# Aggregation of a graph layer: gathered rows become the stationary operand, one-hots of 80 nodes the moving one

## What is computed

```
deg     = max(segment_sum(1, dst), 1)                 # edges per node, first block
agg[v]  = sum over edges e with dst[e] = v of  ew[e] * table[src[e], :]
wdeg[v] = sum over edges e with dst[e] = v of  ew[e]  # weights per node
```

## Time and profile before

| | us |
|---|---|
| median of three runs | 3854.28 |
| span of the profiled execution | 4334.5 |
| PE busy in it | 2842.8 (66%) |
| POOL busy | 2524.5 (58%) |
| DVE busy | 1865.2 (43%) |
| ACT busy | 795.6 (18%) |
| first aggregation, from the first gather on | 106 to 1271 |
| second | 1815 to 2971 |
| third | 2977 to 4185 |

### The profile page before, as it was taken

The page is one execution under the profiler, slowest core; times in us unless marked ns, Lnnn a source line. Parts: engine busy times, 40 slices in busy tenths (PEclk is TensorE's granted clock), DMA queues, the critical chain, the costliest instruction groups (busy, mean ns, idle before and its releaser), DMA issues. The chain is left out here.

```text
span 4334.5 us, 42515 instructions
## 1 busy us (share of the span) xinstructions
PE 2842.8 (66%) x12338; PEld 2151.9 (50%) x12338; DVE 1865.2 (43%) x5797; ACT 795.6 (18%) x1977; POOL 2524.5 (58%) x2689
## 2 busy tenths in 40 slices
PE   3577767777777566646656656555476767767678
PEld 2455545555544544435545545444354555555557
DVE  6343446666646823513322222222244444444443
ACT  1111101111113223301111111100022222232230
POOL 4666666666630533666666666665666666666601
PEclk9788879888888788978878778776788888888878
DMA  5333334444432466634333333332333333333305
GB/s 156 101 111 105 108 94 121 124 128 118 120 90 87 151 200 196 208 108 119 116 101 108 108 108 107 102 98 82 89 107 108 106 107 110 103 110 109 104 21 180
DMA packets 279543, 501.74 MB, mean 116 GB/s; under 512 B 59771, under 2 KB 179969, under 8 KB 279162
## 3 DMA queue, kind: packets, MB, share of 16 engines
q0 software_dynamic: 126240, 345.85, 27.7%
q1 hardware_dynamic: 135916, 139.10, 10.4%
q10 hardware_dynamic: 17136, 13.84, 1.0%
HBM read 419.12 MB, written 79.18 MB: 115 GB/s over the span
## 5 line engine op out<-in xcount | busy, mean ns | idle before, releaser
L1401 POOL DMA_INDIRECT g<-d_t,src_i x1568 | 1506.9, 961 | 806.4 <-issue 483.4
L1473 PE MATMUL bank<-g,m 128*128 128x256 f32 (+1 forms) x4704 | 1440.7, 438 | 94.3 <-issue 45.4
L1473 PEld LDWEIGHTS bank<-g,m 128*128 128x128 f32 x4704 | 943.0, 221 | 307.3 <-issue 141.2
L1401 POOL DMA_INDIRECT g<-d_xn,src_i x784 | 766.0, 977 | 389.2 <-issue 223.7
L1426 DVE TENSOR_SCALAR m<-iota,rel_f,ew_f 128x128 f32<-128x128 f32 x2352 | 702.0, 362 | 383.3 <-DMA d_xs<-zero 170.3
L1461 PE MATMUL bank<-ident,s 128*128 128x128 f32 x588 | 144.0, 334 | 438.3 <-ACT s L1407 390.2
L1437 DVE TENSOR_TENSOR accT<-bank,accT 128x256 f32 x294 | 121.9, 415 | 628.8 <-remote 269.8
L1407 ACT ACTIVATE s<-bank 128x256 f32<-128x256 f32 (+1 forms) x294 | 111.7, 380 | 1338.4 <-DMA nb<-d_deg 435.6
L1461 PEld LDWEIGHTS bank<-ident,s 128*128 128x128 f32 x588 | 86.3, 166 | 495.2 <-ACT s L1407 425.9
L1425 DVE TENSOR_SCALAR eq<-iota,rel_f 128x128 bf16<-128x128 f32 x784 | 227.5, 290 | 182.9 <-remote 140.3
L1435 DVE TENSOR_TENSOR dinv<-bank,dinv 2x128 f32 x98 | 27.1, 276 | 319.4 <-remote 310.0
(11 more groups left out here) (386 smaller groups left out, 4235.9 us busy)
## 6 DMA issues: line engine op xcount, KB each, us to landing
g<-d_t,src_i POOLq DMA_INDIRECT x1568
side_xn<-d_xn SPq DMA_DIRECT2D x96, 256.0 KB
g<-d_xn,src_i POOLq DMA_INDIRECT x784
d_swT<-wkv SPq DMA_DIRECT2D x48, 256.0 KB
swT<-d_swT SPq DMA_DIRECT2D x24, 512.0 KB, 3.7
xt<-d_xs POOLq DMA_DIRECT2D x80, 128.0 KB, 2.9
d_ys<-y ACTq DMA_DIRECT2D x80, 128.0 KB, 2.5
x<-in_x SPq DMA_DIRECT2D x24, 256.0 KB, 2.8
```

The source lines that it names most:

```text
L1401: pool.indirect_dma_start(g[n % RING][:, u, 0:D], None, table, bass.IndirectOffsetOnAxis(ap=k.src_i[:, t:t + 1], axis=0)).then_inc(gathere ...
L1473: ins = pe.matmul(b[:, 0:GW], m[o][:, u, :], g[r][:, u, :], start=(u == 0), stop=(u == GT - 1 and not count))
```

## The change

With the roles of the operands swapped a product forms features x nodes directly. `g` is stationary, in two halves of 128 features, and the one-hot moves, 80 nodes wide (WIN = 80). Both halves of the sum and the two rows of counts stand side by side in one bank, [0:80], [80:160] and, in the first aggregation, rows 0 and 1 of [160:240]. The counts come from two narrow stationary tiles: `first_row` (fp32, column 0 is one) with the moving `m`, `second_row` (bf16, column 1 is one) with the moving `eq`. Banks 0, 1 and 7 take turns, so PE may be two groups ahead of DVE's `finish`. ACT's copy, PE's transposes, the tiles `s` and the ones in `g` are gone; `finish` waits for the group's own products and adds straight from its bank.

```diff
--- before.py
+++ after.py
@@ -27,7 +27,8 @@
 AW = D + 2
-WIN = 128
+WIN = 80
+ACCS = (0, 1, 7)
...
@@ -1362,20 +1363,18 @@
 
     k = kit
     RING, ONEHOTS = 4 if count else 5, 3
-    GW = D + 1 if count else D
-    SW = GW + 1 if count else D
     with Stage(nc, kit) as st:
         side = side_of(st, a, d)
-        g = [st.sb(f"g{r}", [P, GT, GW]) for r in range(RING)]
-        m = [st.sb(f"m{r}", [P, GT, P]) for r in range(ONEHOTS)]
-        eq = [st.sb(f"eq{r}", [P, GT, P], BF16) for r in range(ONEHOTS)] if count else []
-        s = [st.sb(f"s{h}", [P, SW]) for h in range(2)]
+        g = [st.sb(f"g{r}", [P, GT, D]) for r in range(RING)]
+        m = [st.sb(f"m{r}", [P, GT, WIN]) for r in range(ONEHOTS)]
+        eq = [st.sb(f"eq{r}", [P, GT, WIN], BF16) for r in range(ONEHOTS)] if count else []
+        first_row, second_row = (st.sb("first_row", [P, 2]), st.sb("second_row", [P, 2], BF16)) if count else (None, None)
...
         gathered = [[st.pool_dma(f"gathered{r}_{h}") for h in range(2)] for r in range(RING)]
-        m_done, multiplied, copied, window_turned, acc_added, ones_set = (
-            st.sem(n) for n in ("m_done", "multiplied", "copied", "window_turned", "acc_added", "ones_set"))
+        m_done, multiplied, acc_added, rows_blank, rows_set = (
+            st.sem(n) for n in ("m_done", "multiplied", "acc_added", "rows_blank", "rows_set"))
@@ -1401,17 +1400,7 @@
                     pool.indirect_dma_start(g[n % RING][:, u, 0:D], None, table, bass.IndirectOffsetOnAxis(ap=k.src_i[:, t:t + 1], axis=0)).then_inc(gathered[n % RING][u // 4], 16)
 
         def main_act(act):
-            def copy(n):
-                wait(act, multiplied, 2 * (n + 1))
-                wait(act, window_turned, n - 1)
-                act.activation(s[n % 2][:], k.bank[n % 2][:, 0:SW], ACT.Copy).then_inc(copied, 1)
-            for i in range(ROUNDS):
-                for slot in range(2 * GT):
-                    if slot == 1 and 0 < i <= NB:
-                        copy(2 * i - 1)
-                    if slot == 9 and i < NB:
-                        copy(2 * i)
-                    at_step(side.act, slot, i)
+            sides(side.act)
 
         def main_dve(dve):
             def prepare(n):
@@ -1422,23 +1411,26 @@
                 for u in range(GT):
                     t = n * GT + u
                     if count:
-                        dve.tensor_scalar(eq[r][:, u, :], k.iota[:], k.rel_f[:, t:t + 1], None, ALU.is_equal)
-                    ins = dve.tensor_scalar(m[r][:, u, :], k.iota[:], k.rel_f[:, t:t + 1], k.ew_f[:, t:t + 1], ALU.is_equal, ALU.mult)
+                        dve.tensor_scalar(eq[r][:, u, :], k.iota[:, 0:WIN], k.rel_f[:, t:t + 1], None, ALU.is_equal)
+                    ins = dve.tensor_scalar(m[r][:, u, :], k.iota[:, 0:WIN], k.rel_f[:, t:t + 1], k.ew_f[:, t:t + 1], ALU.is_equal, ALU.mult)
                 ins.then_inc(m_done, 1)
 
             def finish(n):
                 base = dve.value_load(k.base_i[0:1, n:n + 1], min_val=0, max_val=N)
-                wait(dve, window_turned, n + 1)
+                window = k.bank[ACCS[n % 3]]
+                wait(dve, multiplied, 2 * (n + 1))
                 wait(dve, acc_added, n)
                 if count:
                     to = k.dinv[0:2, bass.ds(base, WIN)]
-                    dve.tensor_tensor(to, k.bank[7][0:2, D:D + WIN], to, ALU.add)
+                    dve.tensor_tensor(to, window[0:2, C * WIN:(C + 1) * WIN], to, ALU.add)
                 at = k.accT[:, :, bass.ds(base, WIN)]
-                dve.tensor_tensor(at, chunks(k.bank[7]), at, ALU.add).then_inc(acc_added, 1)
+                dve.tensor_tensor(at, window[:, 0:C * WIN].rearrange("p (c n) -> p c n", c=C), at, ALU.add).then_inc(acc_added, 1)
             if count:
-                for r in range(RING):
-                    ins = dve.memset(g[r][:, :, D:D + 1], 1.0)
-                ins.then_inc(ones_set, 1)
+                dve.memset(first_row[:], 0.0).then_inc(rows_blank, 1)
+                dve.memset(second_row[:], 0.0).then_inc(rows_blank, 1)
+                dve.wait_ge(rows_blank, 2)
+                dve.memset(first_row[:, 0:1], 1.0).then_inc(rows_set, 1)
+                dve.memset(second_row[:, 1:2], 1.0).then_inc(rows_set, 1)
             prepare(0)
             prepare(1)
             for i in range(ROUNDS):
@@ -1452,27 +1444,21 @@
                     at_step(side.dve, (h, "b"), i)
 
         def main_pe(pe):
-            def turn_window(n):
-                wait(pe, copied, n + 1)
-                wait(pe, acc_added, n)
-                if count:
-                    pe.transpose(k.bank[7][0:2, D:D + WIN], s[n % 2][:, D:SW], k.ident[:])
-                for c in range(C):
-                    ins = pe.transpose(k.bank[7][:, c * P:(c + 1) * P], s[n % 2][:, c * P:(c + 1) * P], k.ident[:])
-                ins.then_inc(window_turned, 1)
-
             def tile(n, u):
-                r, o, b = n % RING, n % ONEHOTS, k.bank[n % 2]
+                r, o, b = n % RING, n % ONEHOTS, k.bank[ACCS[n % 3]]
+                last = u == GT - 1
                 if u == 0:
                     wait(pe, m_done, n + 1)
-                    wait(pe, copied, n - 1)
+                    wait(pe, acc_added, n - 2)
                     if count:
-                        wait(pe, ones_set, 1)
+                        wait(pe, rows_set, 2)
                 if u % 4 == 0:
                     wait(pe, gathered[r][u // 4], 64 * (n // RING + 1))
-                ins = pe.matmul(b[:, 0:GW], m[o][:, u, :], g[r][:, u, :], start=(u == 0), stop=(u == GT - 1 and not count))
+                pe.matmul(b[:, 0:WIN], g[r][:, u, 0:P], m[o][:, u, :], start=(u == 0), stop=False)
                 if count:
-                    ins = pe.matmul(b[:, GW:SW], eq[o][:, u, :], k.ones_b[:, 0:1], start=False, stop=(u == GT - 1))
+                    pe.matmul(b[0:2, C * WIN:(C + 1) * WIN], first_row[:], m[o][:, u, :], start=False, stop=False)
+                    pe.matmul(b[0:2, C * WIN:(C + 1) * WIN], second_row[:], eq[o][:, u, :], start=False, stop=False)
+                ins = pe.matmul(b[:, WIN:C * WIN], g[r][:, u, P:C * P], m[o][:, u, :], start=False, stop=last)
                 if u % 4 == 3:
                     ins.then_inc(multiplied, 1)
             for i in range(ROUNDS):
@@ -1480,8 +1466,6 @@
                     n = 2 * i + slot // GT
                     if n < NG:
                         tile(n, slot % GT)
-                    if slot % GT == 3 and 0 < n <= NG:
-                        turn_window(n - 1)
                     at_step(side.pe, slot, i)
 
         def tiles_of_edges(eng, body):
```

More of the change, by code:

```diff
@@ L1500, in stage_aggregate @@
         gw, r = flat(g[1]), flat(g[2])
-        ma, mb = m[0][:, 0, :], m[1][:, 0, :]
+        ma, mb = (t[:].rearrange("p u n -> p (u n)")[:, 0:P] for t in m[0:2])
         gidx = st.sb("gidx", [P, 1], I32)
```

## The result

| kernel | median us | range, runs | against the kernel before, 95% interval |
|---|---|---|---|
| before | 3853.0 | 3841.5 to 3855.9, 6 | |
| after | 3870.4 | 3865.4 to 3877.8, 6 | 1.0052 (1.0041 to 1.0062) |

A forecast was written before the change was run, and what follows sets the result against it. POOL's gathers, 1.25 us apart and never waiting inside an aggregation, were taken as the bound. -3.0 us for the stage ends and -2.5 for the port gave 3854.3 - 5.5 = 3849 us, range 3824 to 3872.

The forecast's parts named there:

- the ends of the stages: Chain behind each aggregation's last gather gets shorter: -1.1 us in the second, -1.2 third, -0.7 first, sum -3.0.
- the port: SBUF port pair shared by DVE and POOL: narrower one-hots delay gathers less, -2 to -10 us, taken as -2.5.
- the price of the count products: First aggregation on PE: two f32 pairs 0.14 us and one bf16 product 0.08, making a tile 0.66 us, at most 0.77.
- the end of the first stage: Behind the first aggregation's last gather: -1.1 us for the chain, +0.4 for the last half group's tiles, -0.7 in all.
- rival B: Third stage: L1332 or L1317 newly meets a gather each round, up to 25 us, 3874 (half the rounds 3862); chance 0.14.
- rival C: First stage: narrow products keep PE's clock low, 31 us a round against POOL's 20.0, total 3957 to 4388; chance 0.05.
- the profile's gaps: POOL's 478 to 490 us of late gathers in the earlier profile, read as belonging to that profiled execution only.
- pairs 0.11 us apart: PE's load-and-matmul pairs with 128 stationary, 80 moving columns: the load sets the pace, 0.11 us each, 0.44 a tile.
- What PE, ACT and DVE save in mid-stage: Inside the aggregations their work per round stays below POOL's 20.0 us, so savings there shorten nothing by themselves.
- "18.2 us" a round: First aggregation: PE's work per round of 16 gathers, 16.4 + 1.8 us, still under POOL's 20.0.
- the opposite: Rival that shifted DVE operations miss the gathers and free the port, up to 50 us: 3826 or 3835; chance 0.33.
- The 50 us of meetings: All gathers' excess over 0.945 us each in the earlier profile, taken as the most a freer port could gain.

The follow-up runs named there:

- b0: The kernel before, unchanged, measured and profiled again for a trace without gaps: ratio 1.0012, profiled span 3850.9 us.
- batch: Against after: the two count products of all 8 tiles of a group issued together ahead of the group's last product; 3862.8 us, 1.0029 against before.
- s100: Against the kernel before: only the first aggregation (with the counts) in the new form, the second and third as before; ratio 1.0025.
- both: Against after: the edits of batch and psum together; 3843.6 us, 0.9985 against before.
- psum: Against after: the slice softmax's small tiles mx and tot moved from SBUF to PSUM; 3856.7 us, 1.0013 against before.
- wide: Against after: first_row and second_row with 128 columns instead of 2, products at the same place; single execution, 3869.3 us beside 3851.2 for before.

## Why the prediction was wrong

In the prediction's own sum, -5.5 us was -3.0 for the ends of the stages and -2.5 for the port. Measured, in the two traces, were +7.7 and -0.4 behind the stages and +10.9 inside the third, +18.2 in all. **The steps that failed** are the price of the count products, from which the end of the first stage was reckoned, and the port, where a gain was forecast and a loss came. That 3870 us lies within 3824 to 3872 is luck: the upper bound was rival B alone at its full 25 us, while B brought 10.9 and the rest came from what C describes, which the range left out.

**Right.** POOL's gathers 1.25 us apart bound all three stages; the profile's gaps were its own; a load with 128 stationary columns sets PE's pace (pairs 0.11 us apart, 0.45 us a tile against 0.44 forecast). What PE, ACT and DVE save in mid-stage shortens nothing: ACT's busy time in the second stage fell from 138 to 99 us and the time by 0.03 +- 0.1%. Behind the last product of the second stage the sum follows almost at once:

```profile
2658.70 0.64 PE L1461 MATMUL bank<-m,g 128*128 128x80 f32 x2
...
2659.47 0.33 DVE L1427 TENSOR_TENSOR accT<-bank,accT 128x160 f32 x1 [11.34 <-PE bank L1461]
```

By the modelled end of the product (2659.34) it is 0.13, where 1.05 us lay before. The 1.1 and 1.2 us forecast for the ends of the second and third stages were not seen whole, though. From the last gather to the last sum it is 7.3 us in after and 6.0 in b0, for the products there ran at the lower clock; but over all traces this distance is 5.0 to 7.3 us with the new second stage (nine traces) and 6.0 to 8.3 with the old (four), and in the third stage 8.1 to 9.3 against 8.6 to 9.7. The gain is there at most in part, and is smaller than the spread between executions.

**Wrong, first: the price of the count products.** "Sum 0.44 + 0.14 + 0.08 = 0.66 us", at most 0.77, was 0.87. Each term was right by itself, as batch shows (0.45, 0.14, 0.05). The step that failed took durations from rows in which a product stands among its like, and added them for an order in which 2-column and 128-column loads alternate. The switch costs 0.23 us a tile. By the prediction's own way of adding, "18.2 us" a round would have been 16.4 + 16 x (0.87 - 0.55) = 21.5, above the 20.0 of the gathers; the trace has 972.9 / 49 = 19.9 us of PE a round against 16.0 in b0, since the clock was 0.92 and the sum had not taken off the transposes that went (0.33 us a group at full clock in b0's trace). Either way PE had no room left, least of all at the lower clock. Even this would have cost little in mid-stage, since full-clock stretches make it up: during 79 us at 0.50 from 468 us on, after's sums fell from 12.9 to 30.4 us behind their gathers, and by 803 us they were at 14.0 again.

**Wrong, second: the end of the first stage,** put at -1.1 + 0.4 = -0.7 us and measured as +7.6 to the start of the second. It was reckoned at full clock, and as if PE came to the last gather with nothing left over. Rival C named the mechanism and was given 0.05, because it was priced as if the clock had to stay low for a fifth of the stage or more. It stayed low for the last 52 us of the gathers, and that was enough (s100 has this loss alone, and in both it is gone), for nothing comes after it that could hide it. The premise was fulfilled in the other stages too: their mean clock fell from 0.90 to 0.76 and from 0.94 to 0.79, but there PE had room. What keeps the clock low was not tested. That PE never pauses isn't enough for it, as two stretches of after show:

```profile
468.00:547.00 79.00, 79.00 (x360) 60.83 (x359) 25.72 (x118) 0.60 (x1) 59.81 (x64) 0.50 0.39 112
547.00:813.00 266.00, 265.15 (x1957) 214.81 (x1957) 196.42 (x583) 41.19 (x96) 202.02 (x211) 1.00 0.50 143
```

PE has no pause in the first and one of 0.7 us, at 812, in the second. In the second it ran 380 side products of 128 or 256 columns beside the edge products, in the first only 30, and from 1052 us to the last sum of the stage none, only products of 80 columns. That is in line with rival C's mechanism. The falls themselves came behind pauses: each of the eight in after's first aggregation stands within 2.1 us behind a pause of PE of 0.7 to 2.2 us. The last one, with the clock at 0.50 from 1052.1 us on:

```profile
1051.53 0.42 PE L1457 MATMUL bank<-m,g 128*128 128x80 f32 x2 [1.88 <-DMA g<-d_xn,src_i]
```

Not every pause is followed by a fall (one of 1.4 us at 935 us is not), and no run changed the pauses or the side products alone, so both stay observations.

**Wrong, third: the port.** -2.5 us was forecast, on the ground that narrower one-hots free POOL. In the second stage they may: its gathers lose 4.4 us instead of 6.6. But in the third stage rival B came to pass, with its mechanism and place, for 10.9 of its 25 us; its condition, that the operation cover the point 0.12 us after a gather's start, lacks that it must have begun before the gather. Its chance was 0.14 beside 0.33 for the opposite, which asked that the time of meetings fall by half. The 50 us of meetings behind that rival were too many as well: b0 has 34.9 in its three stages, and the rest stood only in the profile with the gaps. The one meeting of the earlier trace rows gave the price, but I didn't count how many there were: b0 shows that the old kernel lost only 6.5 us to the two operations in this stage, so there was far less to gain from a new phase (6.5) than to lose (45 rounds x 2 operations x 0.5 = 45 us). I gave the larger chance to the smaller side.

The Trainium skill (SBUF — State Buffer, "SBUF: two separate sides") says of a DVE operation with two SBUF inputs and a GpSimd operation that whichever starts first holds the port pair that they share for the whole instruction. The traces agree for the operations that begin before a gather, which then takes longer by the time from its start to their end, less 0.12 us, and psum agrees: with one input in PSUM the same 0.69 us cost no gather anything, 5.4 us of excess instead of 22.2. That an operation which begins behind the gather's start be blocked until its end is not seen: it takes its 0.69 to 0.72 us all the same.

## What to carry to other kernels

Price an instruction in the order in which it will run: on PE, small products of another stationary width belong together, not between wide ones. Where an engine works at a fixed pace set by another, compute its need per period at its lower clock too, since behind the last period nothing hides what is left over. And where DVE and GpSimd run side by side, look for DVE operations with two SBUF inputs before moving anything: putting a small operand in PSUM removes the collision, while shifting the schedule only draws another lot.

## What was not expected of the hardware

- Alternating 2- and 128-column stationary operands, f32, 80 moving: 0.87 us a tile; grouped: 0.64. With all loads 128 columns wide, still alternating with the count products: 0.74.
- A product with 128 stationary and 80 moving columns at 1.2 GHz: 0.21 us a pass (0.85 a tile of four in batch, 1118.52 - 1118.09 = 0.43 for two in wide), 0.11 at 2.4 GHz: where the load sets the pace, the pace follows the clock.
- With the narrower products the granted clock was lower although PE was busy for longer: 687 us at 0.90 in the second stage before, 769 us at 0.76 after (a part of the 769 is the lower clock itself).
- A gather that begins 0.05 us or more behind the start of a DVE operation of 0.69 us lasts up to 1.47 us if that has two SBUF inputs, and 0.95 us if one of them is in PSUM. Begun less than 0.044 us before the gather, or behind its start, the same operation costs it nothing.
- In after's first aggregation PE held the full clock for 264 us without a pause (547 to 811), and lost it each time within 2.1 us behind a short pause.
